# All key blocks placed by GpSimd's DMAs with the residual at once, and the first group's keys spread by two queues after a rearranged prologue

## The chip, the cores and the metric

One core of one Trainium2 chip. The metric is the device time of one execution in microseconds; the kernel before took 326.47 us (median of 3 runs, 326.3 to 327.18).

## What is computed

The input x is 8 images of 64 channels, 32 by 32, float32. First a window attention block: layernorm over channels, attention in windows of 8 by 8 pixels with 8 heads of depth 8 and a relative position bias, projection, residual, then a second layernorm and an MLP (64 to 256 to 64, gelu) with residual. Then a block that makes its convolution weights from the data: a 1x1 convolution, a gate over channels, depthwise convolutions with kernels 3, 5 and 7 on the first 32 channels, a 1x1 convolution and a residual. The change touches the attention only:

```python
xn = _layernorm(xc, ln1_scale, ln1_bias)
qkv = xw @ w_qkv + b_qkv
attn = jnp.einsum('bnhd,bmhd->bhnm', q * scale, k)
attn = attn + bias.transpose(2, 0, 1)[None]
attn = jax.nn.softmax(attn, axis=-1)
out = jnp.einsum('bhnm,bmhd->bnhd', attn, v).reshape(Bn, N, C)
xc = xc + x_attn
```

## The kernel before

The 128 partitions hold 64 channels of two halves of the batch (bh). The 4096 columns are worked through in NG = 8 groups of G = 512 columns; a group holds NW = 8 window pairs ("windows" w = 0 to 7), each with T = 64 pixels. Values are split into a rounded high part and a low part (the rest), so that fast matmuls in fp32r keep the precision.

Each group passes through stages: centered (subtract the mean, PE L787), square, variance (PE L787 again), Ln and Exp for the inverse deviation (ScalarE L561, L563), normalise (DVE L1194), queries, keys and values (PE L814, L809, L819), evacuation of their high parts (ScalarE L572, L581) and low parts (DVE L1198, L1203). Then the keys are spread twice:
- k_heads: SP copies each head's rows by one DMA, 8 per group (spread_keys, L379). With q_blocks it makes a first score pass in one precision (scores_for_max, PE L840), whose maxima are reduced by DVE (take_maximum, L1216), transposed (L846) and spread over minus_max (L1222 to L1225).
- k_blocks: a block-diagonal form for the real scores. Its early half (windows 0 to 3) is placed by four DVE copies (early_key_blocks, L1210), its late half by four GpSimd DMAs (late_key_blocks, L461); for group 0 four larger GpSimd DMAs place both (L453).

q_heads are spread by SP, 8 DMAs for each half of a group's windows (L391); q_blocks by four GpSimd DMAs (L469). The real scores (PE L864 and L867, seven matmuls a window) start from minus_max; ScalarE takes Exp (L601), PE multiplies with the values (L883), DVE turns and divides. The projection (L891) is evacuated by ScalarE (L605), added to x by DVE (add_residual, L1254), rounded by ScalarE (high_of_x1, L609), its low part made by GpSimd (low_of_x1, L287), and goes into centered2 (PE L787) for the second layernorm.

The stages are pipelined over steps g = 0 to 7 (steps 2 to 5 in loops): step(g) does the scores of group g, the maxima of nxt = g + 1, the layernorm, keys and queries of far = g + 2, and residual and second layernorm of prev = g - 1; DVE also finishes an older group. Each engine's order is written out by hand, in a function step of its own, and engines wait for one another by semaphores. A DMA adds 16 to its semaphore.

The order around the change. DVE in a step: low parts of normed2, early key blocks, residual, turn_values, normalise, eight maxima, spread_maxima, divisions, normalise2, k_low, turn, divide, q_low. ScalarE: Exp of windows 0 to 4 with evacuations between, inverse_deviation, high_of_x1, Exp 5, square 2. PE: scores 5, maximum windows 0 and 1, scores 6, centered2, maximum windows 2 and 3, scores 7, maximum windows 4 to 7, keys, transpose_maxima, variance2, values, queries. GpSimd: low_of_square, low_of_x1, low_of_square2, late key blocks, low_of_x, query blocks.

The prologue brings group 0 to its first score. DVE makes the low part of x (L287), scales weights, normalises (L1194), puts the bias into k_heads (bias_with_keys, L1172) and q_heads (bias_with_queries, L1180), with high and low parts of the two bias tables (L1185, L1190). GpSimd builds pick (L435). ScalarE fills constants into k_blocks (L660), rounds x, evacuates, and puts the bias into the late windows of q_heads (late_bias, L675). SP issues spread_keys(0), spread_queries(0, 0) and (0, 1), spread_keys(1), the loads of x for the rest, then the queries and keys of each further group.

```python
        MAX_BANKS = (MAX0, MAX0 + 1, MISC1)
            def step(g, nxt, far, prev, par):        # tensor, cut
                scores(g, 5)
                maximum_pass(0, 1)
                scores(g, 6)
                if prev is not None:
                    centered2(prev)
                maximum_pass(2, 3)
                scores(g, 7)
                maximum_pass(4, 5, 6, 7)
```

After the attention come the MLP and the convolutions (PE L1088), which the change doesn't touch.

## Time and profile before

| | us |
|---|---|
| median of 3 runs | 326.47 |
| lowest, highest | 326.3, 327.18 |
| the profiled execution | 329.44 |
| its span | 327.6 |
| PE busy in the span | 289.0 (88%) |
| DVE busy | 246.9 (75%) |
| ScalarE (ACT) busy | 203.0 (62%) |
| GpSimd (POOL) busy | 92.0 (28%) |

The profile is of one execution; the span runs from its first to its last instruction, and 1.8 us of the execution's time lie around it. PE's busy time counts pipelined matmuls. PEld is PE's loading of weights, SPq the issuing of DMAs by SP's queue. "[0.58 <-POOL parts L287]" behind a row says that the engine stood idle 0.58 us before it, until that group of instructions released it.

### The profile page before, as it was taken

The page shows a single profiled execution, that of the slowest core. Times are in us where ns is not written, and L with a number is a line of the kernel's source. Part 1 is how long each engine was busy: PE and PEld are TensorE (multiplying, and loading weights), DVE is VectorE, ACT ScalarE, POOL GpSimd, SP SyncE. Part 2 cuts the span into 40 slices and gives each one's busy share as a digit, 9 for nine tenths or more (in the row PEclk, how much of TensorE's full clock was granted, in tenths as well). Part 3 has the DMA queues.
Part 4 walks back from the last instruction along what each step waited for, and adds up shares of the span by engine and source line. Part 5 has one row for each costly group of instructions (what it writes and reads, how often), then busy time and mean ns, then how long its engine had stood idle before and what let it go on. Part 6 is the DMA issues. An engine that isn't in the chain of part 4 may idle for free.

```text
span 327.6 us, 6201 instructions
## 1 busy us (share of the span) xinstructions
PE 289.0 (88%) x2314; PEld 209.9 (64%) x2314; DVE 246.9 (75%) x484; ACT 203.0 (62%) x343; POOL 92.0 (28%) x116
## 2 busy tenths in 40 slices
PE   0577897989999898999979897899899999999994
PEld 0345684768868687776868653354477777777772
DVE  3686589579899898989977354779999999976211
ACT  5587643838658585765735697977961755754500
POOL 4063316255263464534250611131310000000000
PEclk9995999999999999999998999999999999999998
DMA  6961356224132331413320000392007568766911
GB/s 152 179 141 44 79 138 119 57 73 89 34 90 63 72 75 36 103 55 71 74 73 13 2 1 2 65 211 58 0 2 145 126 129 179 142 139 144 191 32 32
DMA packets 16380, 28.10 MB, mean 86 GB/s; under 512 B 5088, under 2 KB 11744, under 8 KB 16352
## 3 DMA queue, kind: packets, MB, share of 16 engines
q1 hardware_dynamic: 13792, 22.72, 30.5%
q0 software_dynamic: 1984, 4.20, 7.3%
q10 hardware_dynamic: 576, 0.81, 1.0%
q8 instruction: 18, 0.29, 0.4%
q14 instruction: 10, 0.08, 0.1%
HBM read 4.22 MB, written 2.10 MB: 19 GB/s over the span
## 4 chain that ended last, share of the span: by engine, by line
PE 61%; DVE 12%; SPq 9%; ACT 6%; DMA 4%; issue 4%; POOL 2%; DVEq 0%; ACTq 0%
PE psum L1088 26%; PE psum L867 8%; SPq L391 5%; PE psum L787 5%; SPq L379 4%; PE psum L1012 3%; DVE maxima L1216 3%; PE psum L864 3%; PE psum L1000 3%; DMA k_heads<-k_parts 3%; POOL parts L287 2%; PE psum L809 2%; PE psum L840 2%; PE psum L883 2%; DVE k_blocks L1210 2%
## 5 line engine op out<-in xcount | busy, mean ns | idle before, releaser
L1088 PE MATMUL psum<-shifted,conv_w 128*128 128x512 f32 x336 | 86.6, 419 | 0.0
L1088 PEld LDWEIGHTS psum<-shifted,conv_w 128*128 128x128 f32 x336 | 63.9, 191 | 21.5 <-issue 1.3
L867 PEld LDWEIGHTS psum<-q_heads,k_blocks 128*128 128x128 f32 x384 | 55.4, 191 | 5.9 <-issue 2.8
L867 PE MATMUL psum<-q_heads,k_blocks 128*128 128x256 f32 x384 | 56.6, 283 | 0.0
L1216 DVE TENSOR_REDUCE maxima<-psum 128x8 f32<-128x512 f32 x64 | 40.4, 682 | 11.1 <-PE psum L840 10.0
L601 ACT ACTIVATE probs<-psum 128x512 f32<-128x512 f32 x64 | 37.4, 603 | 15.8 <-PE psum L867 15.6
L287 POOL TENSOR_TENSOR parts<-x,parts 128x256 fp32r<-128x256 f32 (+1 forms) x21 | 19.4, 938 | 59.2 <-ACT parts L609 33.7
L787 PE MATMUL psum<-parts,center_average 128*128 128x512 f32 x64 | 23.1, 443 | 13.7 <-DVE parts L287 9.4
L864 PE MATMUL psum<-minus_max,pick 128*128 128x512 f32 x64 | 32.3, 504 | 2.4 <-DMA q_heads<-q_parts 1.9
L840 PE MATMUL psum<-k_heads,q_blocks 128*128 128x256 f32 x128 | 23.3, 308 | 8.1 <-DMA k_heads<-k_parts 5.5
L273 ACT CAST conv_w<-conv_w 32x896 fp32r<-32x896 f32 x31 | 29.1, 938 | 0.4
L1476 DVE SCALAR_TENSOR_TENSOR x<-psum,weights,x 64x512 f32<-64x512 f32 x16 | 12.0, 749 | 21.0 <-PE psum L1088 20.9
L287 POOL TENSOR_TENSOR parts<-square_logvar,parts 128x512 fp32r<-128x512 f32 x14 | 18.0, 1287 | 31.3 <-ACT square_logvar L556 16.0
L840 PEld LDWEIGHTS psum<-k_heads,q_blocks 128*128 128x128 f32 x128 | 19.4, 204 | 11.6 <-issue 6.3
L730 ACT CAST conv_w<-whole_w 128x896 fp32r<-128x896 f32 x8 | 7.5, 936 | 27.5 <-DVE whole_w L1451 18.9
L514 POOL TENSOR_TENSOR images<-square_logvar,images 128x512 fp32r<-128x512 f32 x8 | 10.7, 1339 | 42.0 <-ACT images L713 42.0
L787 PEld LDWEIGHTS psum<-parts,center_average 128*128 128x128 f32 x64 | 10.4, 200 | 17.0 <-issue 9.6
L703 ACT ACTIVATE hidden<-psum,mlp_bias 128x512 f32<-128x512 f32 x32 | 19.5, 699 | 2.5 <-PE psum L1000 2.4
L1000 PE MATMUL psum<-normed,mlp_w 128*128 128x512 f32 x64 | 18.4, 425 | 1.4 <-ACT hidden L703 1.4
L883 PEld LDWEIGHTS psum<-probs,v_blocks 128*32 128x32 f32 x1024 | 15.5, 112 | 5.2 <-issue 4.9
L1210 DVE CAST k_blocks<-k_parts 32x512 fp32r<-32x512 f32 x28 | 12.9, 459 | 7.4 <-PE psum L867 7.0
L461 POOL DMA_DIRECT2D k_blocks<-k_parts x28 | 16.1, 583 | 7.4 <-PE psum L867 6.8
(143 smaller groups left out, 486.9 us busy)
## 6 DMA issues: line engine op xcount, KB each, us to landing
shifted<-images SPq DMA_DIRECT2D x32, 332.5 KB, 5.5
q_heads<-q_parts SPq DMA_DIRECT2D x128, 32.0 KB, 1.8
k_heads<-k_parts SPq DMA_DIRECT2D x64, 32.0 KB, 2.3
out<-x SPq DMA_DIRECT2D x8, 256.0 KB, 4.9
q_blocks<-q_parts POOLq DMA_DIRECT2D x28, 64.0 KB, 2.5
k_blocks<-k_parts POOLq DMA_DIRECT2D x28, 64.0 KB
x<-in_x SPq DMA_DIRECT2D x6, 256.0 KB, 5.1
x<-in_x SPq DMA_DIRECT2D x4, 128.0 KB, 4.8
```

The lines of the kernel that those rows point to most:

```text
L273: ins = copy(conv_w[bh][shift * KS:(shift + 1) * KS, part, :, C:], w[(shift - 1) * KS:shift * KS, :, 0:C])
L287: return engine.tensor_tensor(low, whole, high.bitcast(F32), ALU.subtract)
L601: act.activation(probs[:, w, :], psum[:, PROB0 + w % 2, :], ACT.Exp).then_inc(S["ac_probs"], 1)
L703: act.activation(hidden[:, par, m, :], psum[:, HIDDEN0 + m, :], ACT.Gelu, bias=mlp1_bias[:, m % 2:m % 2 + 1]).then_inc(S["ac_gelu"], 1)
L787: ins = pe.matmul(psum[:, bank, :], center_average[:, which, :], parts[:, part, :], start=part == 0, stop=part == 1)
L840: ins = pe.matmul(max_bank(w)[:, hh * G // 2:(hh + 1) * G // 2], q_blocks[:, hh, w, :], of_half(k_heads, hh)[:, :, w * T:(w + 1) * T], sta ...
L864: pe.matmul(bank, pick[:, w, :], minus_max[:, :, :], start=True, stop=False)
L867: ins = pe.matmul(bank[:, hh * G // 2:(hh + 1) * G // 2], k_blocks[:, hh, w // (NW // 2), k_part, w % (NW // 2), :], of_half(q_heads[:, q_ ...
L883: ins = pe.matmul(psum[32 * j:32 * j + 32, PV, column:column + T], v_blocks[:, par, at:at + 32], probs[:, w, head * T:(head + 1) * T], sta ...
L1000: ins = pe.matmul(psum[:, HIDDEN0 + m, :], mlp1_w[:, part, f * 128:(f + 1) * 128], normed2[:, bh, bass.ds(n * G, G)], start=part == 0, sto ...
L1088: ins = pe.matmul(psum[:, CONV0 + bh, :], conv_w[bh][:, w_part, t, :], img[:, y:y + H - 1:2, x0:x0 + W], start=t == 0 and w_part + part == ...
L1216: dve.tensor_reduce(maxima[:, w * NH:(w + 1) * NH], max_bank(w).rearrange("p (h t) -> p h t", t=T), AX.X, ALU.max).then_inc(S["dv_max"], 1)
```

## The change

- In the steps, the four DVE copies of the early key blocks are taken out. GpSimd's function key_blocks(n, par, s) places both halves by four DMAs each, the early ones after low_of_next_square and before low_of_x1. Each half has a semaphore of its own.
- DVE so comes to add_residual right after the low parts of normed2. ScalarE does high_of_x1 before inverse_deviation, once the variance of the third group is there. PE does maximum windows 2 and 3 before centered2.
- Prologue, first keys: heads 0 to 3 of group 0 by SP, heads 4 to 7 by GpSimd, with a semaphore of their own; GpSimd's pick waits for the first centered matmul.
- Prologue, DVE: the high part of the second bias table comes before normalise(0); then keys' bias, low bias, queries' bias, q_low, k_low, other_weights, the maxima without a pause, spread_maxima, and only then normalise(1).
- Prologue, ScalarE: key block constants around Ln and Exp; one pass of the late bias before the queries' evacuation, the others after square(1); evacuation of queries and keys of group 1 after the first Exp of step 0.
- Prologue, PE: values(0) after the bias matmuls; variance(1) after window 5 instead of window 1; queries(1) and keys(1) after the first scores of step 0.

```diff
+        def keys_of_head(engine, n, h, done):
+            engine.dma_start(of_head(k_heads, h)[:, h, :].bitcast(F32).rearrange("p (s c) -> p s c", s=2),
+                             of_head(k_parts, h)[:, n % 2, :, 0, :].bitcast(F32)).then_inc(S[done], 16)
+        FIRST_KEYS_BY_SP, FIRST_KEYS_BY_POOL = range(0, NH // 2), range(NH // 2, NH)
+        def wait_keys_placed(engine, groups):
+            engine.wait_ge(S["k_heads_in"], 16 * (NH * groups - len(FIRST_KEYS_BY_POOL)))
+            engine.wait_ge(S["first_keys_in"], 16 * len(FIRST_KEYS_BY_POOL))
...
 SP, spread_keys
-                for h in range(NH):
-                    sp.dma_start(...).then_inc(S["k_heads_in"], 16)
+                for h in FIRST_KEYS_BY_SP if n == 0 else range(NH):
+                    keys_of_head(sp, n, h, "k_heads_in")
 SP, spread_queries
-                    sp.wait_ge(S[f"q_heads_set{half}"], 1 + half)
+                    sp.wait_ge(S[f"q_heads_set{half}"], 1 + 3 * half)
...
 GpSimd
             pool.wait_ge(S["consts_in"], 16)
-            pool.wait_ge(S["center_in"], 16)
+            pool.wait_ge(S["pe_xc"], 1)
             pool.tensor_tensor(pick[:], ...)
-            def late_key_blocks(n, par):
-                pool.wait_ge(S["pe_scores"], NW * n)
+            def key_blocks(n, par, s):
+                pool.wait_ge(S["pe_scores"], NW * (n - 1) + (s + 1) * NW // 2)
                 pool.wait_ge(S["dv_k_low"], n + 1)
                 for hh, bh, r in QUADRANTS:
-                    pool.dma_start(k_blocks[r, hh, 1, ...], k_parts[r, par, 1]...).then_inc(S["k_blocks_in"], 16)
+                    pool.dma_start(k_blocks[r, hh, s, ...], k_parts[r, par, s]...).then_inc(S[f"k_blocks_in{s}"], 16)
             def step(g, nxt, far, after, prev, par):
                 if far is not None:
                     low_of_next_square(far)
+                if nxt is not None:
+                    key_blocks(nxt, 1 - par, 0)
                 if prev is not None:
                     low_of_x1(pool, prev)
                     low_of_square2(pool, prev)
                 if nxt is not None:
-                    late_key_blocks(nxt, 1 - par)
+                    key_blocks(nxt, 1 - par, 1)
             low_of_next_x(1)
+            pool.wait_ge(S["ac_k_high"], 1)
+            pool.wait_ge(S["k_heads_set"], 1)
+            for h in FIRST_KEYS_BY_POOL:
+                keys_of_head(pool, 0, h, "first_keys_in")
             first_key_blocks()
...
 ScalarE, step
                 exponentials(g, 0)
+                if isinstance(g, int) and g == 0:
+                    evacuate_q(1, 1)
+                    evacuate_k(1, 1)
...
                 exponentials(g, 4)
+                if prev is not None:
+                    if far is not None:
+                        act.wait_ge(S["pe_var"], far + 1)
+                    high_of_x1(prev)
                 if far is not None:
                     inverse_deviation(far)
-                if prev is not None:
-                    high_of_x1(prev)
...
 ScalarE, prologue
+            act.wait_ge(S["consts_in"], 16)
+            key_block_constants(0)
             inverse_deviation(0)
-            act.wait_ge(S["consts_in"], 16)
-            for half in range(2): ...
+            key_block_constants(1)
             act.wait_ge(S["x_in0"], 32)
             high_of_x(1)
             act.wait_ge(S["qkv_ready"], 1)
             evacuate_k(0, 0)
+            act.wait_ge(S["dv_rel_high"], 1)
+            late_bias(0, rel_high, 0)
             evacuate_q(0, 0)
             first_query_blocks()
             act.wait_ge(S["v_set"], 1)
             evacuate_v(0, 0)
             square_of_centered(1)
+            late_bias(0, rel_high, 1)
             act.wait_ge(S["dv_rel_low"], 1)
-            late_bias(0, rel_high)
+            for half in range(2):
+                late_bias(1, rel_low, half)
             inverse_deviation(1)
             act.wait_ge(S["x_in1"], 32)
             high_of_x(2)
-            late_bias(1, rel_low)
-            evacuate_q(1, 1)
-            evacuate_k(1, 1)
...
 PE, step
                 scores(g, 0)
+                if isinstance(g, int) and g == 0:
+                    pe.wait_ge(S["dv_normed"], 2)
+                    queries(1)
+                    keys(1)
...
                 scores(g, 6)
+                maximum_pass(2, 3)
                 if prev is not None:
                     centered2(prev)
-                maximum_pass(2, 3)
...
 PE, prologue
-            values(0)
             pe.wait_ge(S["raw_in"], 16)
...
+            values(0)
             centered(1)
             for w in range(NW):
                 scores_for_max(0, w)
-                if w == 1:
+                if w == 5:
                     variance(1)
-            pe.wait_ge(S["dv_normed"], 2)
-            queries(1)
             transpose_maxima(0)
-            keys(1)
...
 DVE, step
-                if nxt is not None:
-                    early_key_blocks(nxt, 1 - par)
                 if prev is not None:
                     add_residual(prev)
 DVE, prologue
             high_of_bias(0, rel_flipped, "dv_rel_flipped")
+            high_of_bias(1, rel_high, "dv_rel_high")
             normalise(0)
             bias_with_keys()
+            low_of_bias()
+            bias_with_queries()
+            q_low(0, 0)
             k_low(0, 0)
-            high_of_bias(1, rel_high, "dv_rel_high")
-            low_of_bias()
-            q_low(0, 0)
-            bias_with_queries()
+            other_weights()
             for w in range(NW):
                 take_maximum(0, w)
-                if w == 3:
-                    normalise(1)
             spread_maxima(0)
-            other_weights()
+            normalise(1)
             q_low(1, 1)
             k_low(1, 1)
```

## Rows read from the trace of the kernel before

**Rows 1.** Page, part 4: chain that ended last, by engine.

```profile
PE 61%; DVE 12%; SPq 9%; ACT 6%; DMA 4%; issue 4%; POOL 2%; DVEq 0%; ACTq 0%
```

**Rows 2.** Stretches: length; busy PE, PEld, DVE, ACT, POOL; PEclk, DMA share, GB/s.

```profile
27.00:35.10 8.10, 7.01 (x24) 4.40 (x23) 6.79 (x13) 5.02 (x9) 2.56 (x5) 0.73 0.10 32
34.91:36.10 1.19, 1.00 (x7) 0.99 (x8) 1.12 (x6) 0.66 (x1) 1.19 (x3) 1.00 0.84 124
94.90:114.60 19.70, 18.62 (x226) 14.64 (x225) 17.95 (x36) 13.53 (x27) 9.80 (x13) 1.00 0.29 68
```

**Rows 3.** Timeline of one loop step: start, us, engine, line, operation.

```profile
102.44 1.71 DVE L1210 CAST k_blocks<-k_parts 32x512 fp32r<-32x512 f32 x4
...
104.18 0.76 DVE L1254 TENSOR_TENSOR x<-square_logvar,x 128x256 f32<-128x256 f32 x2
...
105.67 1.30 POOL L287 TENSOR_TENSOR parts<-x,parts 128x512 fp32r<-128x512 f32 x1 [3.81 <-ACT parts L609]
106.07 1.27 DVE L1216 TENSOR_REDUCE maxima<-psum 128x8 f32<-128x512 f32 x2
...
107.03 0.73 PE L787 MATMUL psum<-parts,center_average 128*128 128x512 f32 x2 [0.58 <-POOL parts L287]
...
108.03 3.91 DVE L1216 TENSOR_REDUCE maxima<-psum 128x8 f32<-128x512 f32 x6 [0.69 <-PE psum L840]
...
109.01 0.88 PE L840 MATMUL psum<-k_heads,q_blocks 128*128 128x256 f32 x6
110.19 2.30 POOL L461 DMA_DIRECT2D k_blocks<-k_parts  x4
...
110.89 1.10 PE L809 MATMUL psum<-normed,qkv_w 128*128 128x512 f32 x2 [0.18 <-DVE maxima L1216]
```

**Rows 4.** Chain of waits: landing of the last first key head.

```profile
23.02 3.36 DMA k_heads<-k_parts
```

**Rows 5.** Timeline of the prologue, all engines.

```profile
5.96 2.46 DVE L287 TENSOR_TENSOR parts<-x,parts 128x256 fp32r<-128x256 f32 x2
6.24 1.90 POOL L435 TENSOR_TENSOR pick<-consts 128x1024 fp32r<-128x1024 f32 x1 [3.63 <-DMA consts<-in_consts]
...
14.37 0.69 DVE L1194 TENSOR_TENSOR normed<-psum,rstd 128x512 f32<-128x512 f32 x1 [0.53 <-ACT rstd L563]
14.97 2.47 DVE L1172 TENSOR_SCALAR k_heads<-normed,consts 128x2048 fp32r<-128x2048 f32 x2
...
17.35 0.69 ACT L572 ACTIVATE k_parts<-psum,qkv_bias 128x512 fp32r<-128x512 f32 x1 [0.41 <-PE psum L809]
...
18.07 0.75 DVE L1198 SCALAR_TENSOR_TENSOR k_parts<-psum,qkv_bias,k_parts 128x512 fp32r<-128x512 f32 x1 [0.63 <-ACT k_parts L572]
...
19.56 3.23 POOL L453 DMA_DIRECT2D k_blocks<-k_parts  x4 [0.85 <-DVE k_parts L1198]
...
21.06 2.88 DVE L1180 TENSOR_SCALAR q_heads<-normed,consts 128x1024 fp32r<-128x1024 f32 x4
...
24.91 2.19 ACT L675 ACTIVATE q_heads<-normed,consts 128x1024 fp32r<-128x1024 f32 x2
...
33.35 0.43 PE L846 MATMUL psum<-consts,maxima 128*64 128x128 f32 x2 [0.43 <-DVE maxima L1216]
...
35.10 0.47 PE L864 MATMUL psum<-minus_max,pick 128*128 128x512 f32 x1 [0.26 <-issue]
...
35.41 0.88 PE L867 MATMUL psum<-q_heads,k_blocks 128*128 128x256 f32 x6
```

**Rows 6.** Timeline: SP's issue of group 1's keys; PE in step 1.

```profile
37.86 5.90 SPq L379 DMA_DIRECT2D k_heads<-k_parts  x8
...
66.22 0.71 PE L840 MATMUL psum<-k_heads,q_blocks 128*128 128x256 f32 x4 [1.00 <-DMA k_heads<-k_parts]
```

**Rows 7.** Timeline of step 6, PE.

```profile
165.01 0.73 PE L787 MATMUL psum<-parts,center_average 128*128 128x512 f32 x2 [0.38 <-POOL parts L287]
```

**Rows 8.** DMA issues: KB each, median us to landing.

```profile
probs<-in_raw SPq DMA_DIRECT2D x1, 192.0 KB, 11.3
```

More of the change, by code:

```diff
@@ L656, in _, with key_block_constants, late_bias @@
             act.dma_start(weights[:, _WAT["vec"][1]:], d["weights"][:, _WAT["vec"][1]:]).then_inc(S["weights_in"], 16)
+            def key_block_constants(half):
+                act.activation(k_blocks[:, half, :, 0], reversal().rearrange("p (s w) t -> p s w t", s=2), ACT.Copy, scale=not_in_half(half)
+                               ).then_inc(S["k_blocks_set"], 1)
+            def late_bias(part, rel, half):
+                late = range(NW // 2, NW)
+                act.activation(query_rows(part, half, late), bias_rows(rel, half, late), ACT.Copy, scale=not_in_half(half)
+                               ).then_inc(S["q_heads_set1"], 1)
+            act.wait_ge(S["consts_in"], 16)
+            key_block_constants(0)
             inverse_deviation(0)
-            act.wait_ge(S["consts_in"], 16)
-            for half in range(2):
-                ins = act.activation(k_blocks[:, half, :, 0], reversal().rearrange("p (s w) t -> p s w t", s=2), ACT.Copy, scale=not_in_half(half))
-            ins.then_inc(S["k_blocks_set"], 1)
+            key_block_constants(1)
             act.wait_ge(S["x_in0"], 32)
@@ L670, in _ @@
             square_of_centered(1)
-            def late_bias(part, rel):
-                late = range(NW // 2, NW)
-                for half in range(2):
-                    ins = act.activation(query_rows(part, half, late), bias_rows(rel, half, late), ACT.Copy, scale=not_in_half(half))
-                ins.then_inc(S["q_heads_set1"], 1)
+            late_bias(0, rel_high, 1)
             act.wait_ge(S["dv_rel_low"], 1)
-            late_bias(0, rel_high)
+            for half in range(2):
+                late_bias(1, rel_low, half)
             inverse_deviation(1)
```

44 lines of the change are left out of this document (16 added, 28 removed).

## The prediction

> **What bounds the kernel now.** I read the chain that ended last first. Half of it lies in the convolutions at the end, which the change doesn't touch; SP's issuing (9%), the landing of key heads, DVE and a few waits come from the attention part [rows 1]. The stretches then divide that part in two. In the loop a step takes 19.70 us, with PE busy for 18.62 and DVE for 17.95: both are nearly full, so only what makes one wait for the other counts. The prologue is sparse, and at its end TensorE's granted clock averages 0.73 [rows 2].
>
> **Loop.** One step in time order [rows 3]: DVE places the early key blocks (1.71 us from 102.44) and only then adds the residual (104.18). After it come ScalarE's rounding of x1 (over by 105.6), GpSimd's low part (105.67 for 1.30) and centered2 on PE, which stood idle 0.58 us for it until 107.03. Two maximum windows, a score window and three more maximum windows follow in PE's order. The fifth maximum (third of the six DVE reductions) can start only after the matmul at 109.01; keys and the transposed maxima hang on the last ones. So 0.58 us per step is on the path, and it is caused by the 1.71 us ahead of the residual and by centered2 standing in front of maximum windows 2 and 3.
>
> **Prologue.** The last key head lands at 26.38 and starts the maxima [rows 4]. The transposed maxima are at 33.35, the first scores at 35.10 [rows 5]. Then a second path rules: SP issues queries, keys (from 37.86, 5.90 us), loads of x, queries, keys almost without pause, and PE waits 1.00 us for their landing at 66.22, in step 1 [rows 6]. What the prologue gains is passed on only as far as that SP chain starts earlier.
>
> **The change, loop part.** Removed: four DVE copies, 1.71 us. Added: four GpSimd issues per step, 2.30 us like the late ones at 110.19 [rows 3]. GpSimd can make them from 101.9 (its low square is over; I take that from the 3.81 us idle before 105.67, which began at 101.86 [rows 3]) until 104.2. Queued behind them is low_of_x1. The residual can start at 102.44 instead of 104.18 and ends at 103.20; ScalarE rounds x1 until 103.85; GpSimd, free at 104.2, ends the low part at 105.5, before PE asks for it (PE would be there at 106.45, where the 0.58 of idle began, and now passes maxima 2 and 3 first, 0.6 us more). Nothing waits for x1_low any more. What is late next: x1's rounding now stands ahead of Ln and Exp instead of behind them. From 103.85 two passes of 512 columns at 0.69 each (as at 17.35 [rows 5]) reach 105.2; normalise is as long, and DVE's next instruction can start some 0.6 after it, so the first maximum comes at 105.8, against 106.07. That is on time by a tenth or two: window 3 needs a bank that the first reduction frees. Hence the whole PE stall comes off, 0.58 us, but little more, as the fifth maximum was PE's to release. Bounds for one step: 0.3 if the reordered ScalarE runs a quarter microsecond later than this, 0.75 if DVE's own idle of 0.69 before the six maxima also counts in part. The early blocks land, at the 3.4 us of a key head [rows 4], by 107.6; the next scores come 19.7 us after this step's, near 114.6, so 7 us cover them. Without that cover the issues and the landing, 5.7 us, would stand on the path. The steps of this pattern are four, steps 2 to 5; step 6, with no third group, has 0.38 of the same stall [rows 7]. Step 1 waits for key heads instead and the reorder gives nothing there, step 0 has no residual. Sum: 4 x 0.58 + 0.38 = 2.7 us (1.6 to 3.4).
>
> **The change, prologue.** (1) DVE's first low part takes 2.46 us while GpSimd's pick runs 6.24 to 8.14; the residual, also two adds of 256 columns, takes 0.76 [rows 3, 5]. Pick is moved behind the first centered matmul, so 1.7 us come off; pick then lies beside the low square and may give back up to 0.8. Net 0.9: normalise could start at 13.5 instead of 14.37. (2) But the copy of the second bias table now stands ahead of normalise, 0.65 us and a wait for its load. No row shows this load's landing. The nearest is the raw block issued right behind it on SP, some 11.3 us from issue to landing, at about 18 [rows 8]. Bounds: not felt at all (in by 12.9, when DVE comes to it) and 18.0. I take 14, nearer the lower end, as raw is issued behind both halves of the table and has the weights beside it, so that its last packets come after them all. Normalise is then at 14.6, 0.2 later than now. (3) Keys follow as now: high keys at 18.2. Half the heads by SP (4 of 8 issues, so the last one 2.6 us earlier), half by GpSimd at 0.58 to 0.81 each (2.30 and 3.23 for four [rows 3, 5]), and 3.36 to landing as in [rows 4]: all there by 23.9 to 24.8, not at 26.38. In the first keys' path GpSimd still has its low part of x before them, which is over by 17. (4) DVE's queue ahead of the first maximum has grown: bias_with_keys ends about 17.6, then the low bias (0.7 to 1.1), bias_with_queries 2.88, q_low and k_low 0.75 each [rows 5], and other_weights (DVE's work from 34.91 to 36.10, 1.2 [rows 2]): free at 24.3 to 24.5. DVE bounds the first maximum as much as the keys. Eight reductions of 0.65 give 29.6, and variance(1), now behind window 5 and behind GpSimd's block issues and its low square, holds the last two up by 0.6: 30.3. The scores start 1.75 later as now (33.35 to 35.10): 32.1, a gain of 3.0. Block landings (issues over at 26.4) are covered. (5) queries(1) and keys(1) were done beside the maxima; now they stand after the first scores, two passes of 1.1 us each [rows 3] on PE's path. High keys of group 1 are there 1.25 (a score window, 0.47 + 0.88 with an overlap of 0.1 [rows 5]) + 2.2 + 0.7 (17.35, evacuation [rows 5]) = 4.2 after the first scores start, at 36.3, and SP can issue them then, its half 1 of the queries being issued by 33.8, since ScalarE's four passes of late bias (2.19 for two [rows 5]) are over by 28.7. Now it starts at 37.86: 1.6 earlier. From there SP's chain is as before to 66.22. PE, with 3.0 gained and 2.2 given back, has 0.8 plus what the removed waits give, and fits under that. Gain passed on: 1.6 us. With the table in by 13 it is 2.5 (normalise then at 13.6, 1.0 earlier than taken; 0.9 of it counted); with the table at 18, 4.0 later than taken, it is 1.6 - 4.0 = -2.4.
>
> The Trainium skill (SBUF — State Buffer, "SBUF: two separate sides") speaks against moving DMAs to GpSimd: while VectorE runs a copy in a 2-port mode, the descriptors can't be written, and the DMA waits. In the loop the copies that would do this are those taken out. In the prologue bias_with_queries would hold GpSimd's four key heads till 21.6; the last would land at about 24.7 and the gain would be 0.3 less. In this trace four block issues beside the same DVE work took 3.23 instead of 2.30 [rows 3, 5], with blocks twice as large, so the delay is partial at most.
>
> **Sum.** 2.7 + 1.6 = 4.3 us. The profiled execution took 329.44 us (span 327.6), 0.9% over the median of 326.47, so it gives 325.1 for itself and 322.2 against the median. After the attention part nothing changes but its start. I count 0.3%, 1 us, as what a measurement of this kernel tells from no change.
>
> **Rivals.**
> (a) The loop's stall only changes its owner: normalise comes too late behind x1's rounding and DVE starts its maxima late. For: only 0.1 us of slack. Against: 1.7 us were taken from DVE. Then only the prologue counts: 326.5 - 1.6 = 324.9. Chance 0.12.
> (b) More than forecast: the table is in early and DVE's idle 0.69 counts: 2.5 + 3.4 = 5.9, giving 320.6; a clock that no longer sinks in the prologue adds a bit, 319.5. Chance 0.13.
> (c) The second bias table lands at 18 and holds normalise(0): prologue -2.4, loop +2.7, so 326.2, no change. Raw's landing [rows 8] speaks for it; against it, raw is issued later and so is an upper bound. Chance 0.08.
> (d) Slower: TensorE's clock. Now it sinks while PE waits for the key heads, and the low stretch lies under DVE's maxima, where it costs little (27 to 35.1: 0.73 [rows 2, 4]). In the changed kernel PE's idle gets shorter but is followed by DVE-bound maxima until 30; if the low stretch (1.2 GHz instead of 2.4) comes later, over step 0's scores, each window's 0.47 + 0.88 = 1.35 us [rows 5] doubles at worst, and with the maxima and values beside it is nearer 0.9 more. Five windows take back the 4.3 gained; it decides from the sixth, and all eight of step 0 give 7.2 - 4.3 = 2.9 more, 329.4, six 327.6. I take 327.6. Chance 0.06.
> That the DMAs don't replace the copies is excluded by the diff.
>
> **How the numbers follow.** Forecast 0.61, a 0.12, b 0.13, c 0.08, d 0.06. Faster: forecast, a and b, 0.86; same: c, 0.08; slower: d, 0.06. The forecast's own bounds are 320.5 (2.5 + 3.4) to 324.5; the range of 319.3 to 325.6 takes in a and b and leaves out c and d.
>
> **What would show it.** Right: no DVE rows of L1210's kind; the stall before centered2 gone in steps 2 to 6 and their period 19.1; first scores near 32, keys of group 1 issued near 36.3, the wait at the first key heads in step 1 still there. A loop period of 19.7 would refute the loop part; normalise(0) after 15.5 the table's landing; a low clock after 32 would show rival d. If steps 0 and 1 together shrink by more than the keys' start, the SP chain was not their bound.

## The result and the profile after

The changed kernel takes 328.27 us (median of 20 runs, 325.78 to 330.82), the kernel before, run beside it, 326.33 us (20 runs, 325.04 to 327.54). The ratio is 1.005, interval 1.0029 to 1.0071: slower by half a per cent, where 322.2 and "faster" were forecast. One of the 20 executions, 330.82 us, was in a slower state and is not in the ratio. The profiled execution took 329.59 us, with a span of 327.8, so it lies 1.3 us above its median, as that of the kernel before (329.44) lies 3.0 above its own. I read it from the loop backwards.

**Loop.** One step in time order, as in [rows 3]:

```profile
104.72 2.30 POOL L470 DMA_DIRECT2D k_blocks<-k_parts  x4
...
105.35 0.76 DVE L1266 TENSOR_TENSOR x<-square_logvar,x 128x256 f32<-128x256 f32 x2
...
106.20 0.62 ACT L624 CAST parts<-x 128x512 fp32r<-128x512 f32 x1 [0.25 <-DVE x L1266]
...
107.03 1.30 POOL L287 TENSOR_TENSOR parts<-x,parts 128x512 fp32r<-128x512 f32 x1
...
108.10 0.69 DVE L1214 TENSOR_TENSOR normed<-psum,rstd 128x512 f32<-128x512 f32 x1 [0.51 <-ACT rstd L578]
108.71 2.48 DVE L1228 TENSOR_REDUCE maxima<-psum 128x8 f32<-128x512 f32 x4
...
109.79 0.63 PE L809 MATMUL psum<-parts,center_average 128*128 128x512 f32 x2
...
111.64 2.48 DVE L1228 TENSOR_REDUCE maxima<-psum 128x8 f32<-128x512 f32 x4 [0.45 <-PE psum L862]
```

The four DVE copies are gone, GpSimd issues their DMAs just before it needs to make x1's low part, centered2 (L809, 109.79) starts with no idle time before it, and four maxima run in one piece where there were two [rows 3]. The stretches give the period, 18.98 us for 19.70 [rows 2]:

```profile
92.65:111.64 18.99, 18.48 (x226) 14.68 (x225) 16.40 (x32) 13.58 (x27) 12.03 (x18) 1.00 0.39 85
111.64:130.62 18.98, 18.48 (x226) 14.66 (x225) 16.39 (x32) 13.56 (x27) 12.06 (x18) 1.00 0.38 84
```

So the loop does what was forecast, and a little more: 0.72 us a step. The loss is before it: PE's first pass over group 2's keys, in step 1, starts at 68.34, not at 66.22 [rows 6], 2.1 us later, and the rest takes 259.5 us (327.8 - 68.34) instead of 261.4.

**Prologue.** The timeline, all engines, for [rows 4 to 6]:

```profile
5.85 0.76 DVE L287 TENSOR_TENSOR parts<-x,parts 128x256 fp32r<-128x256 f32 x2
...
16.46 0.62 DVE L1205 CAST normed<-probs 128x512 fp32r<-128x512 f32 x1 [3.69 <-DMA probs<-in_rel_table]
17.11 0.69 DVE L1214 TENSOR_TENSOR normed<-psum,rstd 128x512 f32<-128x512 f32 x1
...
20.81 2.56 SPq L339 DMA_DIRECT2D k_heads<-k_parts  x4
21.09 2.84 POOL L339 DMA_DIRECT2D k_heads<-k_parts  x4 [4.78 <-ACT k_parts L587]
...
25.23 0.47 PE L862 MATMUL psum<-k_heads,q_blocks 128*128 128x256 f32 x2 [1.43 <-DMA k_heads<-k_parts]
...
29.76 1.22 PE L809 MATMUL psum<-parts,center_average 128*128 128x512 f32 x2 [0.54 <-POOL parts L287]
...
35.09 0.76 PE L883 MATMUL psum<-minus_max,pick 128*128 128x512 f32 x1 [1.61 <-issue]
35.66 1.48 PE L886 MATMUL psum<-q_heads,k_blocks 128*128 128x256 f32 x6
36.94 1.64 PE L836 MATMUL psum<-normed,qkv_w 128*128 128x512 f32 x2
...
38.41 1.02 PE L831 MATMUL psum<-normed,qkv_w 128*128 128x512 f32 x2
```

The reader is to see three things. DVE waits 3.69 us for the load of the second bias table and normalises group 0 at 17.11, not 14.37 [rows 5]. From there to the first scores it takes 17.98 us instead of 20.73, so these start at 35.09, where they started before (35.10). And then the first scores (0.76 and 1.48 us, where [rows 5] has 0.47 and 0.88) and queries(1) (L836, 1.64 us) run slowly, at half clock; keys(1) (L831) has the full clock again. Only then can the keys of group 1 go to SP, at 40.19 instead of 37.86 [rows 6]. SP goes on with loads of x and with queries, almost without pause, and then issues the keys of group 2, for which PE waits in step 1:

```profile
40.19 6.35 SPq L339 DMA_DIRECT2D k_heads<-k_parts  x8
...
68.34 0.72 PE L862 MATMUL psum<-k_heads,q_blocks 128*128 128x256 f32 x4 [1.58 <-issue]
```

The view puts this wait down to "issue". In this kernel PE waits here for two semaphores, and the one it names last (the four heads that GpSimd placed for group 0) had long been reached, so I take the wait to be for the key heads, as the same row of the kernel before says. The landing itself is not in the row.

The stretches of the same profile (length; busy PE, PEld, DVE, ACT, POOL; PEclk, DMA share, GB/s) show TensorE's granted clock low twice. It falls to 1.2 GHz at about 28, 2.7 us after the end of PE's wait of 1.43 us for the first key heads and with two shorter waits of PE between, and is back at about 38. It falls again at about 69, behind the wait of 1.58 us in step 1, until about 72.3:

```profile
27.00:33.00 6.00, 4.19 (x16) 3.04 (x15) 4.37 (x7) 5.75 (x9) 2.69 (x4) 0.58 0.67 131
33.00:39.00 6.00, 4.39 (x13) 2.87 (x13) 2.02 (x4) 0.98 (x2) 1.40 (x2) 0.57 0.11 34
37.00:39.00 2.00, 2.00 (x5) 0.95 (x5) 0.00 (x0) 0.98 (x2) 0.00 (x0) 0.70 0.00 0
66.00:75.00 9.00, 7.03 (x39) 6.11 (x37) 4.98 (x9) 3.17 (x6) 2.47 (x3) 0.81 0.20 53
```

In the kernel before the clock was full again from 33 on, and full in step 1. The twenty executions agree: the three of the changed kernel with a mean clock of 0.989 or more took 325.78 to 326.27 us, and those with 0.969 and 0.970 that count 329.46 and 329.59. That is a relation and not yet a cause, as a longer wait could also lower the clock; the extra matmuls of experiment 5 act on the clock.

### The profile page after: what moved, and what is told of

Its sections match the earlier page's. It is cut to its first block, busy times and chain, and to the rows that moved or that the text cites. A ratio compares the mean times of both kernels' runs of the same rounds, so it can differ in the third digit from the quotient of the medians.

```text
span 327.8 us, 6209 instructions
## 1 busy us (share of the span) xinstructions
PE 289.4 (88%) x2314; PEld 210.7 (64%) x2314; DVE 234.3 (71%) x456; ACT 202.8 (62%) x343; POOL 109.5 (33%) x148
## 4 chain that ended last, share of the span: by engine, by line
PE 76%; DVE 9%; ACT 4%; issue 3%; DMA 3%; POOL 2%; SPq 2%; DVEq 0%; POOLq 0%
PE psum L1108 26%; PE psum L886 14%; PE psum L883 5%; PE psum L902 5%; PE psum L809 5%; DVE maxima L1228 4%; PE psum L1032 3%; DMA probs<-in_rel_table 3%; PE psum L862 3%; PE psum L1020 3%; PE psum L836 2%; PE psum L831 2%; PE psum L910 2%; PE psum L841 2%; PE psum L1044 1%
## 5 line engine op out<-in xcount | busy, mean ns | idle before, releaser
L886 PEld LDWEIGHTS psum<-q_heads,k_blocks 128*128 128x128 f32 x384 | 56.5, 195 | 6.6 <-issue 3.0
L886 PE MATMUL psum<-q_heads,k_blocks 128*128 128x256 f32 x384 | 57.7, 287 | 0.0
L470 POOL DMA_DIRECT2D k_blocks<-k_parts x56 | 32.2, 582 | 8.7 <-PE psum L886 8.7
L883 PE MATMUL psum<-minus_max,pick 128*128 128x512 f32 x64 | 33.0, 515 | 1.9 <-issue 1.6
L809 PE MATMUL psum<-parts,center_average 128*128 128x512 f32 x64 | 23.1, 445 | 10.5 <-DVE parts L287 8.3
L287 POOL TENSOR_TENSOR parts<-x,parts 128x256 fp32r<-128x256 f32 (+1 forms) x21 | 19.1, 925 | 28.5 <-ACT parts L565 18.7
L1246 DVE STREAM_TRANSPOSE by_query<-psum 128x512 f32<-128x512 f32 x16 | 11.3, 709 | 12.8 <-PE psum L902 12.8
L478 POOL DMA_DIRECT2D q_blocks<-q_parts x28 | 16.1, 583 | 9.0 <-ACT q_parts L596 9.0
```

The source lines that it names most:

```text
L287: return engine.tensor_tensor(low, whole, high.bitcast(F32), ALU.subtract)
L470: pool.dma_start(k_blocks[r, hh, s, :, :, bh * T:(bh + 1) * T].bitcast(F32).rearrange("p l w t -> p (l w) t"), k_parts[r, par, s].bitcast( ...
L809: ins = pe.matmul(psum[:, bank, :], center_average[:, which, :], parts[:, part, :], start=part == 0, stop=part == 1)
L883: pe.matmul(bank, pick[:, w, :], minus_max[:, :, :], start=True, stop=False)
L886: ins = pe.matmul(bank[:, hh * G // 2:(hh + 1) * G // 2], k_blocks[:, hh, w // (NW // 2), k_part, w % (NW // 2), :], of_half(q_heads[:, q_ ...
```

## The experiments

Theories: **T**, the second bias table's load holds normalise(0). **K**, queries(1) and keys(1) behind the first scores cost more than they save. **P**, the first keys on two queues help. **D**, part of the price is TensorE's clock. Other letters (C, S, K1 and so on) are explained in the expectation that uses them. All ratios are to the kernel before in the same set (medians 326.5 to 326.8), with their intervals.

**1. The table.** The two halves of T: DVE makes the table's high part later, or its load goes ahead of the rest of x.

```diff
 DVE, table_later
-            high_of_bias(1, rel_high, "dv_rel_high")
             normalise(0)
             bias_with_keys()
+            high_of_bias(1, rel_high, "dv_rel_high")
 SP, table_load_first
-            load_x(0, slice(G, PIX), S["x_in0"])
             load_bias(1, "rel_table")
+            load_x(0, slice(G, PIX), S["x_in0"])
```

> The changed kernel with one edit: DVE copies the high part of the second bias table after bias_with_keys instead of ahead of normalise(0). Theory T (the landing of the second table holds normalise(0), and with it everything to the first scores): DVE's 3.7 us idle ahead of the copy is gone from the path, normalise(0) starts near 13.5 instead of 17.1, the first scores near 32 instead of 35.1, group 1's keys near 37 instead of 40.2; the time falls by 2.5 to 3.5 us against the changed kernel, to about 325, faster than the kernel before by 1 to 2. Rival C (the table's wait is covered; the time went to a low TensorE clock in steps 0 and 1 and to the queries and keys of group 1 behind the first scores): the first scores move by under 1 us and the time stays within 1 us of the changed kernel's 328.3.

> The changed kernel with the two loads of the second bias table issued by SP ahead of the second half of x for group 1, nothing else. Theory T: the table lands earlier by what the 256 KB of x take, 1 to 1.5 us, and the time falls by about 1 us against the changed kernel; group 1's x then lands later, which has some 2 us of cover. Rival C: no difference.

table_later took 325.97 us, ratio 0.9973 (0.995 to 0.9996): 2.3 us under the changed kernel.

```profile
13.35 0.69 DVE L1214 TENSOR_TENSOR normed<-psum,rstd 128x512 f32<-128x512 f32 x1 [0.54 <-ACT rstd L578]
...
33.02 0.77 PE L883 MATMUL psum<-minus_max,pick 128*128 128x512 f32 x1 [1.61 <-issue]
...
38.98 6.04 SPq L339 DMA_DIRECT2D k_heads<-k_parts  x8
```

Normalise is 3.8 us earlier than in the changed kernel, as expected, but the first scores only 2.1 and group 1's keys 1.2, where some 3 us were expected of each: much of the gain is lost on the way (here the clock was at 0.5 from 25 to about 38, and keys(1) had it low as well).

table_load_first took 327.43, ratio 1.0014 (0.9991 to 1.0038), 0.8 us under the changed kernel, about as expected but with intervals that overlap. DVE's wait shrank to a third:

```profile
13.68 0.62 DVE L1205 CAST normed<-probs 128x512 fp32r<-128x512 f32 x1 [1.25 <-DMA probs<-in_rel_table]
```

T holds by the first of the two. Over five profiles with the table ahead of normalise and its load in the old place, DVE's wait was 1.75, 3.44, 3.69, 4.48 and 4.74 us, so the load lands at 14.6 to 17.5, at another time in each execution. The first scores (33.25) and keys (39.24) of table_load_first lie within 0.3 us of those of table_later, and yet its median is 1.5 us above it; why stays open. That table_later beats the kernel before by only 0.3% with a loop 3 us better says that something else costs as much.

**2. Loop and prologue apart.** loop_part is the kernel before with the changes inside the steps; prologue_part is the changed kernel without them.

```diff
 loop_part: in the steps, and in nothing of the prologue
-                    early_key_blocks(nxt, 1 - par)           # DVE
+                    key_blocks(nxt, 1 - par, 0)              # GpSimd
+                    high_of_x1(prev)                         # ScalarE, before inverse_deviation
+                maximum_pass(2, 3)                           # PE, before centered2
```

> The kernel before with the loop part alone (all key blocks by GpSimd, residual at once, x1 rounded ahead of Ln and Exp, maximum windows 2 and 3 ahead of centered2). Both theories: four loop periods of 18.98 instead of 19.70 as in the changed kernel's trace, and a little in step 6: 3 us less than the kernel before, ratio about 0.991. If it is under 1.5 us, the loop's gain is given back at its ends.

> The changed kernel without the loop part (DVE's early copies back, ScalarE's and PE's order of the steps as before), so the prologue part alone. Both theories: slower than the kernel before by the 1.9 us measured plus the loop's 3, about 5 us, 331. If it is near 328, the two parts get in each other's way (GpSimd's early blocks in steps 0 and 1).

loop_part: 323.73, ratio 0.9909 (0.9877 to 0.994), a gain of 3.0 us. prologue_part: 331.53, ratio 1.0125 (1.0089 to 1.0162), a loss of 4.1 us by the ratio (4.8 by the medians). Loss and gain together make 1.1 to 1.8, near the result of 1.6 by its ratio (1.9 by the medians).

**3. The place of queries(1) and keys(1).** Put behind the first scores in loop_part, and put back ahead of them in table_later and in the changed kernel.

```diff
 loop_part_keys_behind: PE (ScalarE's evacuations alike)
-            pe.wait_ge(S["dv_normed"], 2)
-            queries(1)
             transpose_maxima(0)
-            keys(1)
 ... in step 0, behind scores(g, 0)
+                    pe.wait_ge(S["dv_normed"], 2)
+                    queries(1)
+                    keys(1)
 table_later_keys_ahead, keys_ahead_only: the reverse, both behind transpose_maxima(0)
 ... DVE
-            spread_maxima(0)
             normalise(1)
+            spread_maxima(0)
```

> The loop part on the kernel before, plus one piece of the prologue: queries(1) and keys(1) on TensorE, and their evacuation on ScalarE, moved behind the first scores of step 0. Theory K (group 1's keys reach SP's queue late because two 512-column passes and two evacuations stand behind the first scores, at a low TensorE clock, and SP's chain to step 1 passes this on): in the loop part's trace SP issues these keys at 35.9 and the first scores stand at 34.2; with the piece the keys come 5 to 6 us after the first scores, near 39, and the time rises by 2 to 3 us, from 323.7 to about 326. Rival T2 (only the table's landing counted): within 0.8 us of 323.7.

> The changed kernel with the second table's copy behind bias_with_keys (as in table_later, 326.0) and queries(1), keys(1) and their evacuations ahead of the first scores; normalise(1) comes ahead of spread_maxima. Theory K: group 1's keys are issued by SP 2 to 3 us earlier than at 39.0 and the time falls by 1 to 2.5 us, to 323.5 to 325. Rival: the first scores come as much later and nothing is gained, 326.

> The changed kernel with one part undone: queries(1), keys(1) and their evacuations ahead of step 0's first scores again, with normalise(1) ahead of spread_maxima. The second table's high part stays ahead of normalise(0). Theory K (their place behind the first scores costs 3.2 to 3.3 us, whatever the table does): 328.3 - 3.2 = 325.1, ratio to before 0.994 to 0.998; SP issues group 1's keys at 37.0 instead of 40.2, and the wait at group 1's first key heads in step 1 shrinks by as much. Rival (the table's wait and the keys' place hide one another, since either alone already brought a faster kernel than before): 326.5 to 328, ratio 0.999 or above.

loop_part_keys_behind: 327.02, ratio 1.0005 (0.9976 to 1.0033), 3.3 us over loop_part. table_later_keys_ahead: 322.82, 0.9873 (0.9841 to 0.9905), 3.15 under table_later. keys_ahead_only: 324.98, 0.9935 (0.9905 to 0.9964), 3.3 under the changed kernel. Three contexts, one price: K holds, at the upper end of what was expected or above it (2 to 3 us, 1 to 2.5, 3.2). That K and T don't overlap is shown by the edits taken singly: 2.3 and 3.3 us add up to 5.6, and both together gave 5.45 (328.27 to 322.82). SP's issue of group 1's keys in loop_part_keys_behind and in table_later_keys_ahead:

```profile
34.65 0.77 PE L866 MATMUL psum<-minus_max,pick 128*128 128x512 f32 x1 [1.31 <-issue]
...
40.19 5.01 SPq L379 DMA_DIRECT2D k_heads<-k_parts  x8
```

```profile
36.05 5.00 SPq L339 DMA_DIRECT2D k_heads<-k_parts  x8
```

The first scores start at 34.65 and 34.31 in these: the same moment, but the keys leave 5.5 against 1.7 us after it.

**4. Two queues, and pick.** Both on loop_part, then pick put back in the best version.

```diff
 loop_part_two_queues: heads 0 to 3 by SP, 4 to 7 by GpSimd, as in the change
 loop_part_pick
-            pool.wait_ge(S["center_in"], 16)
+            pool.wait_ge(S["pe_xc"], 1)
 best_candidate: table_later_keys_ahead with
-            pool.wait_ge(S["pe_xc"], 1)
+            pool.wait_ge(S["center_in"], 16)
```

> The loop part on the kernel before, plus group 0's keys on two queues (heads 0 to 3 by SP, 4 to 7 by GpSimd). In the loop part's trace PE waits 4.9 us for the first key heads at 24.7 and SP's first issues take 6.6 us. Theory P (the first maxima hang on SP's eight issues): heads land 2 to 2.5 us earlier, and SP gets to the queries earlier; GpSimd's key blocks and its low square follow 2.3 later, which holds variance(1) behind window 1. The time falls by 0.5 to 1.5 us under 323.7. Rival V: the low square behind eight GpSimd issues takes back all of it, and the time is 323.7 or up to 1 us above.

> The loop part on the kernel before, plus GpSimd's pick behind the first centered matmul. In the profile of before DVE's first low part took 2.46 us beside pick, in the loop part's own profile 0.76, as pick there came after it. If the race of the two starts is lost only in some runs, the median moves little (0 to -0.5 us from 323.7) and the spread of the runs gets smaller; if it is lost in most, -1 us or more. The low square beside pick takes 1.44 instead of 0.69 in the changed kernel's trace, so 0.4 to 0.75 us worse in runs in which the race was won before.

> The run table_later_keys_ahead with GpSimd's pick where it was before the change (behind its constants and the centering matrix, not behind the first centered matmul). Theory R (the early pick wins its race with DVE's first low part in most executions and keeps the low square clear, as loop_part_pick showed with +0.9): 322.8 - 0.9 = 321.9, ratio to before 0.984. Rival (with the first keys on two queues the prologue no longer hangs on the low square): 322.8, ratio 0.987. If the race is lost in the profiled execution, the first low part takes 2.4 us instead of 0.76 there.

Two queues: 322.54, ratio 0.9856 (0.9818 to 0.9893), 1.2 us better than loop_part, as expected, with intervals that overlap. The rows of PE's first pass over the key heads, in loop_part and with two queues, speak for P too:

```profile
24.67 1.20 PE L844 MATMUL psum<-k_heads,q_blocks 128*128 128x256 f32 x4 [4.93 <-DMA k_heads<-k_parts]
```

```profile
22.55 0.48 PE L857 MATMUL psum<-k_heads,q_blocks 128*128 128x256 f32 x2 [1.07 <-ACT q_blocks L602]
```

Counted from normalise (12.73 and 14.60) the pass comes 4.0 us earlier, but the first scores only 0.9, so most of it doesn't arrive there. P is likely, not settled. Pick behind the first centered matmul: 324.61, 0.994 (0.9917 to 0.9963), 0.9 worse, with intervals that touch; best_candidate: 322.29, 0.9849 (0.9803 to 0.9894), 0.5 better, within the intervals too. In neither did the move give the 0.9 us counted for it. The reason is in the first rows of the profiles (timeline, all engines). Of eight with the early pick, two show DVE's low part at 2.46 us (the kernel before [rows 5] and loop_part_two_queues, normalise at 14.37 and 14.60) and six at 0.76 (normalise at 12.6 to 13.3), where pick starts once the second of its two adds is under way or over:

```profile
6.01 0.76 DVE L287 TENSOR_TENSOR parts<-x,parts 128x256 fp32r<-128x256 f32 x2
6.66 1.90 POOL L435 TENSOR_TENSOR pick<-consts 128x1024 fp32r<-128x1024 f32 x1 [4.05 <-DMA consts<-in_consts]
```

That is loop_part. The 2.46 us was a race lost in the one execution that I read. With the late pick DVE's low square takes 1.44 instead of 0.69 in each of the nine profiles that have it, and where the table doesn't hold it normalise comes at 13.35 to 13.56: between the race won and the race lost. The Trainium skill (SBUF — State Buffer, "SBUF: two separate sides") says that of a VectorE operation with two SBUF inputs and a GpSimd operation that reads SBUF whichever starts first holds the shared ports for its whole instruction. The rows of the kernel before agree: pick starts at 6.24, between DVE's two adds, and ends at 8.14, and the second add is over at 8.42.

**5. The clock.** Extra matmuls that keep PE busy in the prologue; they write to a free bank, and nothing reads them.

```diff
+            def fill(times):
+                for _ in range(times):
+                    pe.matmul(psum[:, PROB0, 0:128], const("ident"), const("ident"), start=True, stop=True)
             centered(1)
+            fill(5)
             for w in range(NW):
                 scores_for_max(0, w)
+                if w >= 2:
+                    fill(1)
...
+            fill(2)
             transpose_maxima(0)
+            fill(3)
```

> The changed kernel with 11 to 17 extra matmuls of 128 columns in the prologue, into a bank that is free then: five after centered(1), one after each first score window from the third on, and five around the transposed maxima. They add nothing to the result. Theory D (TensorE's clock fell to 1.2 GHz from 27 to 39 since PE was idle before it, and queries(1) and keys(1) pay for it, 3.1 us of passes instead of 2.2): the granted clock from 33 to 39 rises from 0.57 to 0.9 or more, keys of group 1 are issued at 39.2 instead of 40.2, time 1 to 1.5 us shorter, 327.0. Rival D1: the clock stays low, and the extra matmuls cost up to 1 us, 328.3 to 329.3. Rival D2: the clock rises but the time stays, since the keys' place costs by its order and not by the clock: 328.0 to 328.5.

There are 16 of them. The changed kernel with them takes 324.24 us, ratio 0.9918 (0.9884 to 0.9951): 4.0 us less, far more than the 1 to 1.5 expected. The stretches of the filled kernel, for those of the changed one above:

```profile
27.00:33.00 6.00, 5.12 (x35) 4.38 (x35) 5.43 (x11) 4.18 (x7) 2.88 (x4) 1.00 0.50 114
33.00:39.00 6.00, 6.00 (x36) 4.73 (x36) 1.93 (x3) 4.12 (x9) 2.72 (x5) 1.00 0.32 65
66.00:75.00 9.00, 8.50 (x106) 6.10 (x105) 7.69 (x18) 6.16 (x13) 6.00 (x9) 1.00 0.35 79
```

Both low stretches are gone, though nothing was added near the second. Since the matmuls add work and change no order, I put the 4.0 us down to the clock; but the executions of the changed kernel that had nearly the full clock by themselves (325.78 to 326.27) are still 1.5 to 2 us above 324.24, which I can't explain, and in table_later the two executions with a mean clock of 0.998 and 1.0 (325.52 and 325.97) were no faster than the other ten. Group 1's keys now leave 3.6 us after the first scores, not 5.1:

```profile
32.94 0.47 PE L887 MATMUL psum<-minus_max,pick 128*128 128x512 f32 x1 [0.45 <-issue]
...
36.58 5.00 SPq L339 DMA_DIRECT2D k_heads<-k_parts  x8
```

(The profiled execution also had its table early, with a wait of 1.75 us; it is the fastest of the ten, and 1.8 us of its earlier first scores are the table's.) Does the clock cost the other orders as much? The same helper, at places that suit each order, adds 21 matmuls to the kernel before and to loop_part, 13 to keys_ahead_only and 27 to best_candidate.

> The kernel before with 14 extra matmuls of 128 columns while PE waits for the first key heads, and seven more beside the maxima and behind keys(1). Theory S (the low clock costs the changed kernel more than the kernel before, since there it lies only under DVE's maxima, as it does not in the changed kernel, where queries(1) and keys(1) run at it behind the first scores): the filler gives the kernel before 1 to 2 us, 324.6 to 325.6, against the 4.1 it gave the changed one, and with a full clock in both the two kernels differ by under 1 us (changed 324.2). Rival S1 (the low clock costs both the same): before drops by 4 us to 322.5, and the change costs 1.7 us at a full clock as well. Rival S2: no gain, ratio above 0.999.

> The run keys_ahead_only with the filler of the run filler (without the three behind the transposed maxima). Theory K1 (the place of queries(1) and keys(1) behind the first scores cost 3.3 us, half of it the order, half the clock): with a full clock in both, ahead is 1.5 us better than behind, 324.2 - 1.5 = 322.7. Rival K2 (the whole cost of the place was the clock): 324.2, the same as the run filler. Rival K3 (it was all order): 324.2 - 3.3 = 321.

> The run loop_part (the change's part in the steps alone) with the filler of before_filler. Theory S: as for the kernel before, 1 to 2 us, 323.7 - 1.5 = 322.2. Rival S1: 4 us, 319.7. Rival S2: none, 323.7.

> The run best_candidate with some 28 extra matmuls of 128 columns: seven before keys(0), four behind queries(0), six before the first scores for the maxima, one after each of those, two before the transposed maxima. Theory D (TensorE's clock stood at 0.5 from 21 to 33 in that run, under maxima, queries(1) and keys(1)): clock 0.9 or more there, group 1's keys issued at 33.2 instead of 34.9, 322.3 - 1.7 = 320.6, ratio to before 0.981. Rival: DVE's maxima hold that stretch at any clock, gain below 0.5, 322.

| order | without filler | with filler | ratio with it |
|---|---|---|---|
| kernel before | 326.5 | 325.96 | 0.9967 (0.994 to 0.9994) |
| loop_part | 323.73 | 322.43 | 0.9854 (0.9819 to 0.989) |
| changed kernel | 328.27 | 324.24 | 0.9918 (0.9884 to 0.9951) |
| keys_ahead_only | 324.98 | 323.06 | 0.9883 (0.9847 to 0.9919) |
| best_candidate | 322.29 | 321.31 | 0.982 (0.9783 to 0.9857) |

Theory S holds in its main point: the clock costs the order of before 0.6 us (1.1 by the ratio; 1 to 2 was expected) and the changed one 4.0. At a full clock the changed kernel is 1.7 us faster than the kernel before, though the two intervals still touch. The place of queries(1) and keys(1) then costs 1.2 us (324.24 against 323.06), near what K1 said (1.5), but with intervals that overlap, so that K2, by which all of it was the clock, isn't excluded. By the medians about two of its 3.3 us were the clock. best_filler is the fastest version, 1.8% under the kernel before, though its interval overlaps that of best_candidate. It gave 1.0 us and not the 1.7 expected, and its keys of group 1 were not issued earlier, at 34.90 against 34.91: SP was issuing queries until 34.81 there, so that its own queue set the time.

**What the keys' start decides.** SP's issue of group 1's keys, PE's wait for group 2's key heads in step 1, and the time from that issue to the end of the span, in all profiles with the loop part:

| profile | issue | PE's wait in step 1 | issue to end |
|---|---|---|---|
| filler | 36.58 | none | 283.4 |
| keys_ahead_filler | 37.24 | none | 283.4 |
| table_later_keys_ahead | 36.05 | none | 283.7 |
| loop_part_two_queues | 36.92 | none | 284.0 |
| best_filler | 34.90 | none | 284.2 |
| loop_part_filler | 35.64 | 1.25 | 283.8 |
| loop_part_pick | 36.67 | 1.58 | 285.3 |
| loop_part | 35.92 | 1.14 | 285.4 |
| loop_part_keys_behind | 40.19 | 1.57 | 285.4 |
| keys_ahead_only | 38.78 | 0.90 | 285.4 |
| best_candidate | 34.91 | 1.09 | 285.6 |
| table_load_first | 39.24 | 1.60 | 285.9 |
| table_later | 38.98 | 1.07 | 286.0 |
| changed kernel | 40.19 | 1.58, clock 0.81 in 66 to 75 | 287.6 |

The end moves with the issue, and where PE waits it is mostly some 2 us later still. Two parts of the way differ: SP needs 18.6 to 20.2 us from group 1's keys to group 2's, and where PE waits for these its pass over them starts 8.0 to 8.7 us after their issue. From this pass on the rest is 256.9 to 258.0 us in every profile of the table but that of the changed kernel, with its 259.5 and the low clock behind the pass. All five profiles with an issue at 38.78 or later have the wait, but four of the nine with an earlier one have it too, so a late issue isn't its only cause: it is there whenever PE gets to the pass before SP's chain does. And the issue at 40.19 is followed by the same wait in two profiles, but only once by the low clock; what decides that stays open.

## Why the prediction was wrong

It was wrong in sign: 322.2 us, at most 325.6, was forecast, with 0.86 on faster. The working fails in three terms of the prologue and holds elsewhere. The 6.1 us between 322.2 and 328.27 can be laid out by the two profiles: normalise came at 17.11 and not at 14.6 (2.5 us), the first scores 0.5 more behind it than forecast, SP's issue of group 1's keys 0.9 more behind these, and from there to the end it took 287.6 us and not 287.0 (289.7 of the kernel before less 2.7), with the clock low in step 1 (0.6). That is 4.5 us, from 325.1 to the profiled 329.59; the other 1.6 come from the executions that the profiles show, 3.0 us above the median before and 1.3 after.

- **Loop part: right.** Period 19.1 forecast, 18.98 measured; 2.7 us forecast, 3.0 measured alone. The stall before centered2 went as forecast. DVE's idle time ahead of the later maxima went in part too (0.69 before [rows 3], 0.45 now), which was the upper bound's argument. The residual starts 105.35, 2.75 us ahead of normalise, where it stood 1.31 ahead of it. Rival a is out.
- **Step (2), the table: the term that was furthest off.** "I take 14" for the landing; it was 16.4 in this profile and 14.6 to 17.5 over five. I had bounds of 12.9 and 18.0 and chose near the lower one by the order of issue. Normalise came at 17.11, which by the prediction's own test ("after 15.5") refutes that value. Rival c, at 0.08, was this mechanism. Measured price against a copy out of the way: 2.3 us.
- **Step (5), the two passes behind the first scores: the choice that cost most.** The sum had 4.2 us from first scores to SP's issue, all at full clock, and then compared issue times (36.3 against 37.86). Measured: 5.1 us in the changed kernel, mostly at half clock, 6.0 in table_later and 3.6 at full clock with the filler. The length at full clock was even a little generous; that the gains of (1) to (4) would be there first, and that the clock would be full, was wrong. Without the step the issue comes 1.5 to 1.8 us behind the first scores (38.78 against 37.27, 36.05 against 34.31). The place was never set against the same kernel without it, only against the kernel before: 3.15 to 3.3 us, three times.
- **Rival d, the clock, at 0.06:** its mechanism came, at another place. It was priced on step 0's score windows, 0.9 us each, six or more of them; the low stretch in fact ended at about 38 and lay over the first window and queries(1), and so ahead of SP's chain, and a second one came in step 1. Worth 4.0 us by the filler. That its 327.6 lies 0.7 from the result is luck.
- **Step (1), pick:** against the execution that I read the term was right (normalise at 13.35 in table_later, 13.5 forecast). But its 1.7 us were a lost race; in most executions there was nothing to take, and 0.7 on the low square was added. This is also part of why that execution was 3.0 us over its median. I took the sum off the median all the same, and should have asked which term of it was made of that excess.
- **Steps (3) and (4): right.** From normalise to first scores 17.5 us were forecast (14.6 to 32.1), 17.98 measured, at half clock from 28 on. The key heads were to be in 9.3 to 10.2 us after normalise; PE started on them after 8.1. Two queues alone are worth 1.2 us, within the noise of the two runs. GpSimd's four issues took 2.84 us beside bias_with_queries, between the 2.30 and 3.23 of [rows 3, 5], and PE starts on the key heads at 25.23, 1.4 us after the end of the copies, at 23.84. So the delay that the Trainium skill (SBUF — State Buffer, "SBUF: two separate sides") names was partial here at most; issues held for the whole of the copies don't show.

With T and K undone the kernel takes 322.82 us, near the forecast of 322.2. This is partly chance: that kernel has the two passes in another place than the forecast's path, and no gain from pick. What it shows is that the change is slower by two of its moves, and faster without them.

## What to carry to other kernels

A load that no row shows should be taken at the late end of its bounds when a whole prologue is queued behind it, and a copy that nobody needs soon doesn't belong ahead of the instruction on which everything hangs. Before work is moved behind something "since its path has slack", look for who it feeds: here queries(1) and keys(1) feed the queue that issues DMAs one after another for the next 30 us, and what starts late there is late in step 1 (the keys of group 2). A duration in a sparse stretch is tied to the clock that the stretch before it leaves behind, so price it at both levels; and check an unusually long row against a second execution, if there is one, before counting on its removal.

## What the runs showed of the hardware that was not expected

- 16 matmuls of 128 columns whose results nothing reads made a kernel 4.0 us faster (328.27 to 324.24), where 1 to 1.5 were expected. The granted clock rose from 0.57 to 1.00 in 33 to 39 and also, without any filler there, from 0.81 to 1.00 in step 1, where PE's wait for key heads vanished. The Trainium skill (TensorE: Matmul & The Clock Gate, "HAM oscillation — how this bites in real kernels") describes a loop whose work starts at the low clock each time after a wait for DMA. The trace agrees in part: both low stretches of the changed kernel lie behind a wait (1.43 us by its row for a DMA, 1.58 us as argued above), but the work behind it started at full clock, and the clock fell 2.7 and 0.6 us into it.
- A wait as long doesn't always bring the low clock: 1.57 us at 68.48 in loop_part_keys_behind and 1.60 us at 67.10 in table_load_first were followed by a full clock, 1.58 us at 68.34 in the changed kernel by 0.81 (mean of 66 to 75).
- The landing of one load of the bias table differed by 2.9 us between executions (14.6 to 17.5); issued ahead of the second load of x it landed at 13.7 in the one profile, and the median fell by only 0.8 us.
